# The third norm's squares and their sum: one ScalarE instruction and a VectorE sum, or eight ScalarE instructions with a sum each

## What is computed

```python
def _layernorm(x, axis=-1, eps=1e-05):
    m = jnp.mean(x, axis=axis, keepdims=True)
    v = jnp.var(x, axis=axis, keepdims=True)
    return (x - m) / jnp.sqrt(v + eps)
...
    h = h + _L1_attn_ref(_layernorm(h, axis=-1), ...)
    h = h + _L1_ffn_ref(_layernorm(h, axis=-1), ...)
...
# _L1_ffn_ref, x_flat being the normed tokens
    gate_logits = x_flat @ Wg + bg + bias
    topk_vals, topk_idx = jax.lax.top_k(gate_logits, TOP_K)
    topk_w = jax.nn.softmax(topk_vals, axis=-1)
    combine = (jax.nn.one_hot(topk_idx, NUM_EXPERTS, dtype=x.dtype) * topk_w[..., None]).sum(axis=1)
    h = jax.nn.relu(jnp.einsum('td,edh->teh', x_flat, W1) + b1)
    y = jnp.einsum('teh,ehd->ted', h, W2) + b2
    out = jnp.einsum('ted,te->td', y, combine)
```

## Time and profile before

| | us |
|---|---|
| median of 3 runs | 1157.5 |
| lowest, highest | 1156.64, 1159.77 |
| the profiled execution | 1158.09 |
| its span | 1156.3 |
| TensorE busy | 1097.3 (95%) |
| ScalarE busy | 792.8 (69%) |
| VectorE busy | 694.9 (60%) |

### The profile page before, as it was taken

One profiled execution on the slowest core, in us unless ns is written; L12 is line 12 of the kernel. 1 busy time (PEld: TensorE's weight loads), 2 busy tenths in 40 slices (PEclk: granted clock), 3 DMA queues, 4 the chain that ended last, 5 costly groups with the idle time before them and its releaser, 6 DMA issues.

```text
span 1156.3 us, 62447 instructions
## 1 busy us (share of the span) xinstructions
PE 1097.3 (95%) x26872; PEld 937.4 (81%) x26872; DVE 694.9 (60%) x3130; ACT 792.8 (69%) x4592; POOL 143.5 (12%) x220
## 2 busy tenths in 40 slices
PE   4799999999999999999999999999898779899998
PEld 2699999999999999999999999999644368823332
DVE  7565455555555555555555554444456659899995
ACT  1466777777777777777777777676568888756664
POOL 4200000000000000000000000000103402331210
PEclk9555555555555555555555555555599989999999
DMA  5000000000000000000000000000000000256675
GB/s 143 8 9 10 9 10 13 9 9 9 10 14 9 9 10 9 9 14 9 9 5 5 4 5 5 5 4 5 3 1 1 1 1 1 78 216 228 247 294 194
DMA packets 30545, 47.20 MB, mean 41 GB/s; under 512 B 12274, under 2 KB 21563, under 8 KB 30268
## 3 DMA queue, kind: packets, MB, share of 16 engines
q1 hardware_dynamic: 30268, 43.21, 11.0%
HBM read 40.84 MB, written 2.36 MB: 37 GB/s over the span
## 4 chain that ended last, share of the span: by engine, by line
PE 86%; DVE 6%; ACT 4%; POOL 2%; issue 1%; SPq 0%; DMA 0%; DVEq 0%; ACTq 0%; POOLq 0%
PE bank L657 44%; PE bank L753 7%; PE bank L1385 6%; PE bank L1680 5%; PE bank L736 5%; PE bank L427 4%; PE bank L526 3%; PE bank L731 2%; PE bank L748 1%; PE bank L1583 1%; PE bank L412 1%; POOL stat L1026 1%; PE bank L1418 1%; PE bank L447 1%; PE bank L1674 1%
## 5 line engine op out<-in xcount | busy, mean ns | idle before, releaser
L657 PE MATMUL bank<-space,whh_hi 128*128 128x8 f16 x16384 | 609.5, 169 | 7.4 <-DVE space L784 4.4
L657 PEld LDWEIGHTS bank<-space,whh_hi 128*128 128x128 f16 x16384 | 528.3, 105 | 25.3 <-DVE space L784 7.4
L784 DVE TENSOR_TENSOR space<-h_f,space 128x16 f16<-128x16 f32 x2048 | 291.4, 176 | 380.4 <-ACT h_f L765 378.8
L765 ACT ACTIVATE h_f<-bank 128x16 f32<-128x16 f32 x2048 | 300.1, 184 | 229.8 <-PE bank L657 222.4
L771 ACT ACTIVATE space<-bank 128x16 f16<-128x16 f32 x2048 | 299.0, 184 | 1.1 <-PE bank L657 1.1
L657 PE MATMUL bank<-space,whh_lo 128*128 128x32 f16 (+1 forms) x2096 | 145.0, 190 | 0.0
L753 PE MATMUL bank<-space,wih_hi 128*128 128x32 f16 x2048 | 137.1, 188 | 0.0
L427 PE MATMUL bank<-onehot,tab 128*128 128x128 f16 x448 | 116.7, 266 | 0.5 <-DVE prepare_cur L477 0.5
L736 PE MATMUL bank<-xr,wih_hi 128*128 128x32 f16 x512 | 109.8, 214 | 0.0
L731 PE MATMUL bank<-ones,bias 128*128 128x32 bf16 x512 | 102.9, 201 | 0.0
L657 PEld LDWEIGHTS bank<-space,whh_lo 128*128 128x128 f16 x2096 | 102.2, 107 | 0.0
(11 more groups left out here) (296 smaller groups left out, 1637.7 us busy)
## 6 DMA issues: line engine op xcount, KB each, us to landing
space<-weights_kept SPq DMA_DIRECT2D x64, 512.0 KB, 7.6
space<-in_x SPq DMA_DIRECT2D x28, 129.0 KB, 3.2
out<-res SPq DMA_DIRECT2D x8, 256.0 KB, 9.7
space<-in_wrec SPq DMA_DIRECT2D x1, 768.0 KB, 4.2
space<-in_wx SPq DMA_DIRECT2D x1, 740.5 KB, 9.5
brec<-in_brec SPq DMA_DIRECT2D x1, 260.0 KB
ew<-in_ew SPq DMA_DIRECT2D x1, 256.0 KB, 4.3
weights_kept<-wturned SPq DMA_DIRECT2D x8, 32.0 KB, 1.8
```

The source lines that it names most:

```text
L657: mm = pe.matmul(own[:, m, :], w[:, k, m * P:(m + 1) * P], steps(h, k), start=False, stop=False, skip_group_check=True)
L765: act.activation(h_f[layer][:, s % 2, :, :], own, ACT.Tanh, scale=scale[layer]).then_inc(s_h[layer], 1)
L784: dve.tensor_tensor(h[layer][:, :, s % RINGS[layer], 1, :], h_f[layer][:, s % 2, :, :], h[layer][:, :, s % RINGS[layer], 0, :], ALU.subtra ...
```

## The change

ScalarE squares the eight tiles one by one, each with a second output (`accum_out`) that is the sum over the tile's 64 columns, written to one column of `stat[:, 2, :]`. The last of the eight raises the semaphore that VectorE's sum raised (`s_var`), for which GpSimd waits. Since the sums are now written by ScalarE, the first of them also waits for the root of the sequence before (`s_rstd`), which read the same place. VectorE's sum remains for sequence 2 alone (y = 0), whose squares are still made by the old function. That leaves five sequences, x = 3 to 7, for the new one.

```diff
+            def third_squares_summed(x):
+                act.wait_ge(s_xc, B + x + 1)
+                act.wait_ge(s_rstd, B + x)
+                for t in range(TT):
+                    ins = act.activation(sq[:, t, :], xc[:, t, :], ACT.Square, scale=D ** -0.5,
+                                         accum_out=stat[:, 2, t:t + 1])
+                ins.then_inc(s_var, 1)
+
...
                 elif step == 2 and y + 2 < B:
-                    third_square(y + 2)
+                    third_squares_summed(y + 2)
...
                     elif step == 3:
-                        third_variance(y + 2)
+                        if y == 0:
+                            third_variance(2)
```

## The result

The changed kernel takes 1159.74 us (median of 14 runs) against 1157.97 us for the kernel before in the same comparison: a ratio of 1.0016, 95% interval 1.0009 to 1.0023, or 1.0 to 2.7 us slower. The forecast was 1159.9 us, +2.4.

The account below looks back on a forecast made before the run. TensorE was taken to bound the expert stage, 17.37 us a sequence. Stalls of 0.89 and 1.68 us less 0.15 for VectorE's sums gave +2.4 on 1157.5, so 1159.9 us; range 1156.8 to 1165.5 us.

Parts of the forecast that it names:

- The bound: Expert stage: TensorE sets the pace at 17.37 us a sequence; taking five sums off VectorE gains only 0.15 us.
- The price of a tile: ScalarE's squares: activation plus accumulator read holds the engine 0.26 us a tile, bounds 0.15 to 0.44; 2.08 us a group.
- The slack and the stalls: ScalarE's longer group delays expert 1's relu beyond its slack, stopping TensorE 0.89 us at x = 3, 0.42 at x = 4 to 7.
- The larger first stall: At x = 3 ScalarE still idles 0.47 us for `xc`, as VectorE has saved nothing yet; stall 0.89 us.
- The sum: Expert stage: stalls of 0.89 and 1.68 us less VectorE's 0.15 us give +2.4 us.
- The signs: Profile after: group of 2.1 us, TensorE waiting for relu 0.9 us once and 0.4 four times, 17.8 us a sequence.
- the marks of 1.7 and 2.3 for the rivals: ScalarE's group under 1.7 us would show a cheap read (chance 0.10), over 2.3 us a dear read (0.34).
- The range: Whole kernel: 1156.8 to 1165.5 us, leaving out the faster case, the lost clock and a tile price over 0.42 us.
- the prediction's formula: TensorE's stalls: 8c - 1.19 us once and 8c - 1.66 four times, less 0.15, with c the price of a tile.
- That `xc` would always be early enough from x = 4 on: VectorE's saved time has `xc` ready when ScalarE's first relu ends, so 0.58 us of ScalarE's idling adds to slack, 1.12 us.
- The clock: Rival: five stalls cost TensorE its clock, 1.5 us each, adding 7.6 us to the forecast, 1167.5 us; chance 0.03.
- the prediction's argument against it: TensorE kept its clock when busy 0.80 of 2 us in 1004 to 1006; stalls are under 1 us in 17.

Follow-up runs that it names:

- the squares a slot later: Changed kernel with ScalarE's group of eight squares one slot later, behind the relu of expert 1: 0.9997 of the kernel before, -0.1 us.
- the sums left out: Kernel before without VectorE's sums for x = 3 to 7, ScalarE's single squaring raising the signal for the root: 1.0001 of the kernel before.
- six tiles: Changed kernel with six tiles summed on ScalarE, the last two squared in one instruction and summed by VectorE: stalls 0.55, 0, 0.47, 0, 0.29 us.
- the kernel squared twice: Changed kernel with a second group of eight squares per sequence into places that nothing reads: 1.0139 of the kernel before, +16.1 us.
- the first seven experiments: Runs with eight pieces without sums, squares a slot later, sums left out, squared twice, centring earlier, six tiles summed, and six tiles with centring earlier: 0.9997 to 1.0139 where given.
- the pieces without sums: Kernel before with the squares of x = 3 to 7 in eight one-tile instructions, no second output, VectorE's sums kept: 1.0006, +0.7 us.
- the centring earlier: Changed kernel with VectorE's centring one slot earlier, right behind the mean; read from its trace alone: a stall of 0.25 us at all five x.

## Why the prediction was right

- *The bound.* TensorE sets the pace, and VectorE's sums were worth 0.15 us over four sequences: shown twice, by the squares a slot later and by the sums left out.
- *The price of a tile.* Taken as 0.26 us between 0.15 and 0.44, measured 0.24 us. The form was as expected, a read behind each activation; its length is 0.19 us, that of the shortest activation in the earlier trace rows, but it holds the engine for 0.09 to 0.10 where I had put 0.11. VectorE's 83 ns would have given 0.23. This is the term that was off most: 2.08 us for a group that measured 1.93 once and 1.91 four times, 0.8 us too much in five.
- *The slack and the stalls.* With the measured groups the step gives 1.93 - 0.54 - 0.65 = 0.74 us at x = 3, where 0.85 was measured, and 1.91 - 0.54 - 1.12 = 0.25 at the four others, where 0.25 was measured. The 0.11 at x = 3 are an error in the slack, which is 0.54 us and not 0.65: four matmuls are 0.86 us ahead of the next four, not 0.92, and TensorE starts 0.05 us after relu's end (1032.28 + 1.10 = 1033.38 and 1033.43 in the changed kernel). That x = 4 comes out all the same is luck. The same 0.11 is too much there, and a third error makes up for it: the 0.58 us of idle time count from the end of the relu before, but the squares can start about 0.12 us ahead of that end, as ScalarE's instructions overlap. The relu in question, before and after the change:

```profile
1046.68 1.11 ACT L1268 ACTIVATE gel<-bank,ebias 128x1024 f32<-128x1024 f32 x1
...
1046.99 1.11 ACT L1276 ACTIVATE gel<-bank,ebias 128x1024 f32<-128x1024 f32 x1
```

  With the change the squares follow the relu's start by 1047.98 - 1046.99 = 0.99 us; before, they could have started at 1046.68 + 0.99 = 1047.67 and started at 1048.37, so the idle time was worth 0.70 us. The slack is (0.54 - 0.11) + 0.70 = 1.13 us, against the 1.12 of the prediction. The larger first stall had the cause given, VectorE's centring.
- *The sum.* 1.85 - 0.15 = 1.70 us by the trace's own stalls, against +2.4 forecast and 1.77 between the medians, inside the interval of 1.0 to 2.7. That the time itself, 1159.74 us, lies 0.2 us from the 1159.9 forecast is in part luck: the kernel before took 1157.97 us in this comparison and 1157.5 in the runs that the forecast started from. The time alone proves little, since no change at all would have been within the stated range; the stalls, the group's length and the place of the wait carry the argument.
- *The signs.* The group lasts 1.91 us where 2.1 was named, between the marks of 1.7 and 2.3 for the rivals; the stalls are 0.85 and 0.25 where 0.9 and 0.4 were; a sequence takes 17.62 us, not 17.8.
- *The range.* Its upper end doesn't fit its own condition: by the prediction's formula 1165.5 us (+8.0) belongs to a tile of 0.40 us; 0.42 would be +8.8 us, 1166.3. Nothing measured comes near it.
- *That `xc` would always be early enough from x = 4 on* held in the changed kernel, but on less ground than the prediction gave. It counted only what VectorE saves, not the DMA of the weights, which stops VectorE once it is ahead (0.98 us in one sequence after the change). With a smaller saving on VectorE, six tiles, the lead failed in two sequences of four.
- *The clock.* The rival's mechanism exists, and a short gap in an otherwise full stretch isn't always free, as the prediction's argument against it had it: of the kernel squared twice, one pause of 1.98 us took the clock. The event cost 3.2 us there, not the 1.5 that the rival reckoned with. With stalls under 0.9 us it didn't come up; the granted clock read 1.00 from 1040 on.

## What to carry to other kernels

An instruction moved to an engine with idle time costs by what is queued behind it: 1.4 us more on ScalarE was free a slot later and cost 0.25 to 0.85 us a sequence where it stood, ahead of the relu that frees a PSUM pair. Splitting an activation to get a sum from each piece costs, here, 0.24 us for a piece of 64 columns, where 64 columns more in one long instruction cost 0.06 ((0.54 - 0.15) us over 448 columns), so the sums are dearer on ScalarE, 1.4 us a sequence, than the 0.59 us that they take of VectorE, and all that can pay is the room on VectorE. And room made on an engine that isn't the bound was worth 0.15 us by itself, and 0.6 to 2.9 us once work from a stretch where that engine is the bound was moved into it.

## What the runs showed of the hardware beyond what I expected

The second output of a ScalarE activation is brought out by an instruction of its own, ACTIVATION_READ_ACCUMULATOR: 186 to 203 ns long, 193 in the middle of 40, and overlapped with its neighbours so that it holds the engine for 0.09 to 0.10 us. On VectorE the like takes 83 ns.

Pauses of the same length don't always take TensorE's clock. Of five pauses of 2.0 to 2.6 us in one execution one did (1.98 us long, while the one of 2.58 did not), at a price of 3.2 us. The wait of 2.1 us near 1020 stands in both kernels and in the first seven experiments: in six of these nine profiled runs the clock fell behind it, as in the earlier trace rows, and in three it did not (the pieces without sums, the sums left out, the centring earlier). Where it held, TensorE then waited 1.44 us for VectorE's gate weights, and what the clock saved was lost again: from the group of eight matmuls ahead of the wait to the second one behind it both the kernel before (1016.26 to 1028.18, clock lost) and the one with the sums left out (1014.59 to 1026.51, clock held) take 11.92 us.
